# Routed expert products on one core: the last nine tiles done by halves of their outputs

## The reference, cut to what matters

```python
y      = einsum('bct,bcd->bdt', x, cond_w[itok])          # 64 blocks of 64x64, 4096 rows of 1024
logits = y @ W_gate + b_gate                              # 8 experts
_, top = top_k(logits, 2)                                 # two experts for each row
y_all  = relu(einsum('bsd,edh->bseh', y, W_e) + b_e)      # 1024 x 1024 for each expert
out    = x + take_along_axis(y_all, top, 2).mean(axis=2)
```

## Time and profile before

| what | value |
|---|---|
| median of 3 runs | 889.98 us (889.56 to 890.32) |
| the profiled execution, its own time | 888.81 us |
| its span in the trace | 887.1 us |
| PE busy | 851.0 us, 96% of the span |
| POOL busy | 446.5 us, 50% |
| DVE busy | 428.5 us, 48% |
| ACT busy | 256.9 us, 29% |
| DMA | 162.47 MB, 200 GB/s of memory traffic over the span |

### The profile page before, as it was taken

One profiled execution on the slowest core, in us unless ns is written; L12 is line 12 of the kernel. 1 busy time (PEld: TensorE's weight loads), 2 busy tenths in 40 slices (PEclk: granted clock), 3 DMA queues, 4 the chain that ended last, 5 costly groups with the idle time before them and its releaser, 6 DMA issues.

```text
span 887.1 us, 16691 instructions
## 1 busy us (share of the span) xinstructions
PE 851.0 (96%) x4154; PEld 674.1 (76%) x4155; DVE 428.5 (48%) x578; ACT 256.9 (29%) x310; POOL 446.5 (50%) x500
## 2 busy tenths in 40 slices
PE   7788899999999999999999999999999999999993
PEld 4344468888888888888888888888888888888883
DVE  6698876847643373335533373336433733333320
ACT  5555412134522252114311331115111511111220
POOL 3002224366566647654665556555655565555411
PEclk9899999999999999999999999999999999999997
DMA  9999698998965686547754594547664655444433
GB/s 335 418 415 351 227 330 265 341 333 251 288 158 109 130 266 136 106 95 196 200 103 93 98 298 101 107 100 213 171 118 95 189 114 109 91 101 97 82 48 47
DMA packets 51034, 162.47 MB, mean 183 GB/s; under 512 B 11594, under 2 KB 11658, under 8 KB 50986
## 3 DMA queue, kind: packets, MB, share of 16 engines
q0 software_dynamic: 24544, 76.74, 40.4%
q1 hardware_dynamic: 20618, 67.79, 21.0%
q10 hardware_dynamic: 5840, 17.57, 5.0%
HBM read 106.74 MB, written 70.52 MB: 200 GB/s over the span
## 4 chain that ended last, share of the span: by engine, by line
PE 88%; DVE 6%; DMA 2%; issue 2%; ACT 1%; ACTq 0%; POOL 0%; DVEq 0%; POOLq 0%
PE psO L606 85%; DVE turned L855 2%; PE psO L547 2%; DMA y_rows<-ys 1%; ACT ys L699 1%; DMA raw<-in_L_cond_weights 1%; DVE w_lo L868 1%; PE psG L559 0%; DVE run_hot L918 0%; DVE place_hot L910 0%; DVE idx_all L884 0%; DVE idx_all L883 0%; DVE idx_all L886 0%; DVE raw L885 0%; PE psL L571 0%
## 5 line engine op out<-in xcount | busy, mean ns | idle before, releaser
L606 PE MATMUL psO<-w_hi,a_hi 128*128 (+1 forms) x1104 | 341.7, 391 | 0.3 <-issue 0.3
L606 PE MATMUL psO<-w_lo,a_hi 128*128 (+1 forms) x1104 | 340.6, 390 | 0.0
L606 PE MATMUL psO<-w_hi,a_lo 128*128 (+1 forms) x1104 | 340.4, 390 | 0.0
L464 POOL DMA_INDIRECT rows<-y_rows,idx_g x248 | 255.7, 1031 | 106.8 <-issue 52.1
L606 PEld LDWEIGHTS psO<-w_hi,a_lo 128*128 128x128 f32 x1104 | 207.5, 188 | 43.4
L606 PEld LDWEIGHTS psO<-w_lo,a_hi 128*128 128x128 f32 x1104 | 207.6, 188 | 43.3
L606 PEld LDWEIGHTS psO<-w_hi,a_hi 128*128 128x128 f32 x1104 | 206.9, 188 | 44.1 <-issue 1.7
L1031 DVE TENSOR_TENSOR a_lo<-ys,a_hi 128x1024 fp32r<-128x1024 f32 x62 | 75.9, 1224 | 115.6 <-ACT a_hi L735 115.6
L723 ACT ACTIVATE ys<-ys 128x1024 f32<-128x1024 f32 x33 | 35.0, 1061 | 258.1 <-DVE ys L993 258.1
L723 ACT ACTIVATE rows<-rows 128x1024 f32<-128x1024 f32 x33 | 35.0, 1061 | 252.7 <-DVE rows L993 252.7
L993 DVE TENSOR_TENSOR ys<-psO,bias 128x1024 f32<-128x1024 f32 x33 | 40.2, 1219 | 124.6 <-PE psO L606 108.3
(11 more groups left out here) (141 smaller groups left out, 337.4 us busy)
## 6 DMA issues: line engine op xcount, KB each, us to landing
raw<-in_L_ffn_W_e SPq DMA_DIRECT2D x56, 512.0 KB, 6.2
y_rows<-ys ACTq DMA_DIRECT2D x32, 512.0 KB, 8.3
out<-in_x SPq DMA_DIRECT2D x14, 1024.0 KB, 9.3
rows<-in_x SPq DMA_DIRECT2D x16, 512.0 KB, 10.1
more_x<-in_x SPq DMA_DIRECT2D x16, 512.0 KB, 11.0
bias<-in_L_ffn_b_e SPq DMA_DIRECT2D x8, 512.0 KB
rows<-y_rows,idx_g POOLq DMA_INDIRECT x248
raw<-in_L_ffn_W_e POOLq DMA_DIRECT2D x4, 512.0 KB, 9.0
```

The source lines that it names most:

```text
L464: pool.indirect_dma_start(out=rows[:, slot, a * DQ:(a + 1) * DQ], out_offset=None, in_=y_parts[0:(1 + TOK) * Q, :], in_offset=bass.Indirec ...
L606: last = nc.tensor.matmul(ps[:, h * BANK:(h + 1) * BANK], a[:, p, k * P:(k + 1) * P], w[:, bass.ds(slot + (k * H + h * BANK), BANK)], star ...
```

## The change

Tiles 60 to 68 (HALVED = SURE - 4 = 60 and up) are done by halves of the outputs. PE does all 24 matmuls of half 0 and reports (s_half), then the 24 of half 1. DVE adds the bias to one half as soon as it is there, ACT rectifies it, and POOL scatters it: 128 pieces of 2 KB for each half, with indices 2i and 2i + 1 into `out` seen as rows of 512. POOL makes these in two small operations, waits for the first half's rectifier, issues its scatter, **waits for that to land** (s_add1), waits for the second half's rectifier and issues its scatter, whose landing counts in s_add as before. PE's loop that asks whether a tile is there now begins at 60; it began at 64.

```diff
+    HALVED = SURE - 4
+    out_halves = out.rearrange("n (h c) -> (n h) c", h=NH)
+        idx_h = sb("idx_h", [P, 2 * OS], U32)
+                def scatter_halves(t):
+                    n, half, m = t
+                    pool.wait_ge(s_add, n * 16)
+                    c = pool.value_load(tile_c[0:1, bass.ds(n, 1)], min_val=0, max_val=COLS - 1)
+                    nc.gpsimd.tensor_copy(idx_s[:, m:m + 1], idx_row[:, bass.ds(c, 1)]).then_inc(s_ixs, 1)
+                    pool.wait_ge(s_ixs, n - (EARLY - 1))
+                    pool.sem_inc(s_step, 1)
+                    nc.gpsimd.tensor_scalar(idx_h[:, m:m + 1], idx_s[:, m:m + 1], 2.0, None, ALU.mult).then_inc(s_ixh, 1)
+                    nc.gpsimd.tensor_scalar(idx_h[:, OS + m:OS + m + 1], idx_s[:, m:m + 1], 2.0, 1.0, ALU.mult,
+                                            ALU.add).then_inc(s_ixh, 1)
+                    pool.wait_ge(s_ixh, (n - (HALVED - 1)) * 2)
+                    pool.sem_inc(s_step, 1)
+                    pool.wait_ge(s_out1, n - (HALVED - 1))
+                    pool.sem_inc(s_step, 1)
+                    pool.indirect_dma_start(
+                        out=out_halves, out_offset=bass.IndirectOffsetOnAxis(ap=idx_h[:, m:m + 1], axis=0),
+                        in_=o_sb[m][:, 0:BANK], in_offset=None, compute_op=ALU.add).then_inc(s_add1, 16)
+
+                    pool.wait_ge(s_add1, (n - (HALVED - 1)) * 16)
+                    pool.sem_inc(s_step, 1)
+                    pool.wait_ge(s_out, n + 1)
+                    pool.sem_inc(s_step, 1)
+                    pool.indirect_dma_start(
+                        out=out_halves, out_offset=bass.IndirectOffsetOnAxis(ap=idx_h[:, OS + m:OS + m + 1], axis=0),
+                        in_=o_sb[m][:, BANK:D], in_offset=None, compute_op=ALU.add).then_inc(s_add, 16)
...
                 with pool.Fori((SURE - 4) // 4, (NT + 3) // 4, 1) as i:
...
-                                                  scatter(tile(i, c))))
+                                                  scatter_halves(tile(i, c))))
...
-                                for h in range(NH):
+                                for h in hs:
...
-                    products(t, psO[m % 2], e, slot)
+                    if halves:
+                        for h, done in ((0, s_half), (1, s_mm)):
+                            products(t, psO[m % 2], e, slot, hs=range(h, h + 1), done=done)
+                    else:
+                        products(t, psO[m % 2], e, slot)
...
+                def relu_halves(t):
+                    n, half, m = t
+                    for h, before_it, after_it in ((0, (s_bo1, n - (HALVED - 1)), s_out1), (1, (s_bo, n + 1), s_out)):
+                        at = slice(h * BANK, (h + 1) * BANK)
+                        act.wait_ge(*before_it)
+                        nc.scalar.activation(o_sb[m][:, at], o_sb[m][:, at], ACTF.Relu, scale=0.5).then_inc(after_it, 1)
...
+                def finish_halves(t):
+                    n, half, m = t
+                    e = needed(n)
+                    dve.wait_ge(s_add, (n - (OS - 1)) * 16)
+                    dve.wait_ge(s_bias, e * 16 + 16)
+                    for h, before_it, after_it in ((0, (s_half, n - (HALVED - 1)), s_bo1), (1, (s_mm, n + 1), s_bo)):
+                        dve.wait_ge(*before_it)
+                        V.tensor_tensor(o_sb[m][:, h * BANK:(h + 1) * BANK], psO[m % 2][:, h * BANK:(h + 1) * BANK],
+                                        bias[:, bass.ds((e % 2) * H + h * BANK, BANK)], ALU.add).then_inc(after_it, 1)
```

More of the change, by code:

```diff
@@ L226, in build @@
         s_from = sem("s_from")
+        s_half, s_bo1, s_out1, s_add1, s_ixh = sem("s_half"), sem("s_bo1"), sem("s_out1"), sem("s_add1"), sem("s_ixh")
         s_run, s_fill2, s_list = sem("s_run"), sem("s_fill2"), sem("s_list")
@@ L593, in ranks, with products @@
                     last.then_inc(s_rank, 1)
-                def products(t, ps, e, slot, ks=range(KD), hooks={}):
+                def products(t, ps, e, slot, ks=range(KD), hooks={}, hs=range(NH), done=s_mm):
                     n, half, m = t
@@ L611, in products @@
                     if ks[-1] == KD - 1:
-                        last.then_inc(s_mm, 1)
+                        last.then_inc(done, 1)
                 def early_products(t, ks=range(KD), hooks={}):
@@ L622, in early_products, with all_products @@
                     products(tile(0, t), psO[t % 2], 0, 0, ks, hooks)
-                def all_products(t):
+                def all_products(t, halves=False):
                     n, half, m = t
@@ L666, in _ @@
                 all_products(tile(0, EARLY))
-                with pe.Fori(2, SURE // 4, 1) as i:
+                with pe.Fori(2, HALVED // 4, 1) as i:
                     for c in range(4):
@@ L670, in _ @@
                 there = guard(pe)
-                with pe.Fori(SURE // 4, (NT + 3) // 4, 1) as i:
+                with pe.Fori(HALVED // 4, (NT + 3) // 4, 1) as i:
                     for c in range(4):
-                        there(i * 4 + c, lambda: all_products(tile(i, c)))
+                        there(i * 4 + c, lambda: all_products(tile(i, c), halves=True))
             @block.scalar
@@ L793, in ahead, with step @@
                         act.reg_add(reg, reg, 1)
-                def step(i, c, run):
+                def step(i, c, run, last=relu):
                     v = i * 4 + c
                     run(v - 1, lambda: (run(v, lambda: parts(tile(i, c))),
-                                        needed(v - 1), relu(tile(i, c - 1)),
+                                        needed(v - 1), last(tile(i, c - 1)),
                                         run(v, lambda: ahead(v))))
@@ L811, in _ @@
                     for c in range(4):
-                        step(i, c + 1, there)
+                        step(i, c + 1, there, relu_halves)
                 split_to(2 * (E - 1))
@@ L1122, in finish_last, with step @@
                     finish(t, e)
-                def step(i, c, run):
+                def step(i, c, run, last=finish_last):
                     v = i * 4 + c
@@ L1127, in step @@
                                                         run(v + 1, lambda: returned(tile(i, c + 1))))),
-                                        finish_last(tile(i, c - 1)),
+                                        last(tile(i, c - 1)),
                                         run(v, lambda: ahead(v))))
@@ L1148, in _ @@
                     for c in range(4):
-                        step(i, c + 1, there)
+                        step(i, c + 1, there, finish_halves)
                 split_to(2 * (E - 1))
```

## The result

The changed kernel takes **925.0 us** (median of 4 runs, 923.4 to 928.2), the one before 889.8 (889.4 to 890.3). The ratio is 1.041, 95% interval [1.0395, 1.0432]: slower, 35 us of it. The forecast was 920, range 906 to 932.

What follows compares the result with a forecast made beforehand. PE bounds the kernel before; after the change POOL does from tile 60, with 13 exposed landings of 4.0, 18 issues of 1.6, 9 index rounds of 1.75 and 4 gathers of 6.2 us: 920 us, range 906 to 932.

Steps and rivals of the forecast that it cites:

- POOL becomes the bound: From tile 60 on, POOL needs more per tile than PE's 10.88 us and never catches up.
- 13 exposed landings of 4.0: POOL's waits for half scatters to land, 4.0 us each, range 3.4 to 5.3; halving saves 1.3.
- Rival (c): Landing is fixed cost, mostly latency: a half takes 4.7 or more, 9 us more, 929; chance 13%.
- Issues of 1.6: POOL's 18 issues of half scatters take 1.6 us each, ends 1.0 and 2.0.
- Rival (b): POOL's issue costs by bytes or rows, 1.1 in place of 1.6, with quicker waking: 13 us less, 907; chance 20%.
- Indices 1.75: POOL, index copy to issue: 1.75 us with two more small operations and a semaphore round, bounds 1.5 and 1.9.
- Tiles with a gather 15.15, without 12.95: POOL's us per tile behind tile 60: 15.15 for tiles 61 to 64, 12.95 for those without a gather.
- rival (d): POOL's issues slowed by DVE beside them: 0.5 us on nine issues, 4.5 more, 925; chance 8%.
- PE 0, and DVE and ACT halves 0.69 and 0.63: PE's order by halves costs 0; each half bias takes about 0.69 us, each half rectifier about 0.63.
- Late gathers just in time: Tile 68's gather comes late, its a_lo done by 859; PE needs it at 862.6, so PE keeps pace.
- The tail, 7.3 behind the last issue: From the last issue's end to the span's end: 8.63 less 1.3 for the shorter transfer, 7.3 us.
- The gain meant, 2.3 us: Last tile's tail: 1.0 us from half bias and rectifier, 1.3 from a shorter last transfer, if POOL is free.

Runs made afterwards that it cites:

- e3: Kernel before with only the scatter split in two, both behind the full rectifier, the second behind the first's landing: 923.4 us, ratio 1.039.
- e4: The changed kernel, but half 0's landing is waited for ahead of the next tile's indices, not ahead of half 1's issue: 891.5 us, ratio 1.003.
- e1: Kernel before with only PE's matmuls of tiles 60 to 68 ordered by halves and its guard from tile 60: 888.2 us, ratio 0.999.
- e9: Kernel before with 14 guards on POOL behind its last scatter, for which nothing waits: 892.8 us, ratio 1.002.
- e11: Kernel before with 56 guards on POOL behind its last scatter: 898.6 us, ratio 1.008.
- e2: The changed kernel with PE, bias and rectifier by halves, but one full scatter a tile: 887.5 us, ratio 0.998 to before.
- e8: The version of e2 timed again in more rounds: 887.0 us, ratio 0.999 to before.
- e10: The changed kernel with each half's scatters in their own chain, SP asking at the end whether first halves landed: 891.9 us, ratio 1.001.
- e7: The changed kernel with each half's scatters in their own chain, POOL asking at the end in 14 guards: 889.3 us, ratio 1.002.
- e6: The change, its wait between halves too, for tile 68 alone: 892.5 us, ratio 1.004 to before.

## Why the prediction was right, point by point

- **POOL becomes the bound**: right. e3 has the whole loss with nothing but the scatter split, and e4 takes it away with one wait moved.
- **13 exposed landings of 4.0**: 13 were seen, 4.24 between halves and 4.0 ahead of copies; 54.2 us in place of 52. A full landing before took 5.2 to 5.5, so halving saved 1.1 (between halves) to 1.4 (ahead of copies), about the 1.3 read from the flow of the data. The wait between halves is the longer of the two, where the prediction's low end had it as the shorter. The split by the Trainium skill, "DMA: Bandwidth & Descriptors" (Anatomy of one DMA), 0.6 saved and 4.7 left, isn't what the trace shows. Rival (c), the landing as a fixed cost of 4.7 or more, falls with these 4.0 to 4.2.
- **Issues of 1.6**: right. First halves 1.62 to 1.78, second 1.56 to 2.17. Rival (b), an issue that costs by its bytes, falls: 2 KB rows cost what 4 KB rows do.
- **Indices 1.75**: right for eight tiles (1.68 to 1.75 from copy to issue), 2.57 for tile 60, where the copy itself took 1.00 (it began while DVE's a_lo was running).
- **Tiles with a gather 15.15, without 12.95**: 15.6 and 13.1. Of the 2.5 us that the four tiles with a gather are over, 1.0 is the landings, 1.0 two second issues of 2.05 and 2.17 which began while DVE's a_lo was running (863.52 and 863.03 in the rows above): rival (d), in a small size. The gather's own part, 25.0 in place of 4 x 6.2, is right by luck: it began 0.6 us before the end of the issue ahead of it and not 0.45 behind, but its copy took 0.8 in place of 0.2 and two of its issues, beside a_lo as well, 1.95 and 1.64.
- **PE 0, and DVE and ACT halves 0.69 and 0.63**: right; 0.687 and 0.632 are the means after, and e1 shows PE's 0.
- **Late gathers just in time**: right, but with 0.9 us in hand (a_lo of tile 68 at 864.26, PE due at 865.2) where the prediction had 3.6 (859 against 862.6).
- **The tail, 7.3 behind the last issue**: this step failed. It is 8.4 (918.14 to 926.5). The data did end earlier: the rows below are half microseconds behind the last issue (columns as in the earlier trace rows), three of after, where the flow is over by 920.8, 2.7 us behind the issue, and one of before, where it is over by 882.4, 3.9 behind. So 1.3 us of transfer are saved, and the end comes only 0.3 earlier. That POOL's queue has a share in the end is shown by e9 and e11; why 8.4 are left, where that queue alone would leave 7.5, is not.

```profile
918.50:919.00 0.50, 0.00 (x0) 0.00 (x0) 0.00 (x0) 0.00 (x0) 0.00 (x0) 0.50 1.16 66
...
920.00:920.50 0.50, 0.00 (x0) 0.00 (x0) 0.00 (x0) 0.00 (x0) 0.00 (x0) 0.50 1.00 180
920.50:921.00 0.50, 0.00 (x0) 0.00 (x0) 0.00 (x0) 0.00 (x0) 0.00 (x0) 0.50 0.16 25
```

```profile
882.00:882.50 0.50, 0.00 (x0) 0.00 (x0) 0.00 (x0) 0.00 (x0) 0.00 (x0) 0.50 0.21 33
```

The profiled span is 7.9 us over the sum of 918.6. By place: 2.6 are there before tile 60 is reached (784.19 of the earlier trace rows is 786.82 here), 1.1 at tile 60 itself, 2.5 in the four tiles with a gather, 0.6 in the rest of the chain, 1.1 in the closing. The first is a matter of this execution in part: its 928.2 is the longest of the four runs. None of the prediction's signs of being wrong showed: POOL waits for ACT at no half issue of tiles 65 to 68, and the pairs stand 5.75 us apart or more.

The gain meant, 2.3 us, was also too large by its second part: 1.0 from bias and rectifier is there (e2, e8), the 1.3 from a shorter last transfer mostly isn't (e10: 1.3 in all, where 2.3 was named).

## What to carry to other kernels

Before a transfer is split, count the waits that its issuer will stand in: each piece that must land before the next is issued costs the whole way there and back, here 4.2 us for half the data where the full one had 5.4, and an engine at 50% busy time can be full. Waits belong in chains, each piece behind the one that it really conflicts with (e7, e10), and as late in the queue as the conflict allows (e4). And what stands behind the last issue on POOL's queue delayed the end of the program, even where nothing waited for it (e9, e11).

## What the runs showed of the hardware that was not expected

- The accumulating indirect DMA takes POOL 1.6 us to issue for 128 rows, of 2 KB or of 4 KB; the gather of 128 rows of 1 KB takes 1.0. In the traces of before and after, from 500 us on, longer ones (up to 2.4 and 2.0) are found only where the issue began while one of DVE's subtractions (a_lo, w_lo) was running; all others took 1.56 to 1.67 and 0.94 to 1.04.
- Behind the end of POOL's last issue the span has 8.5 to 8.6 us with a full scatter (before, e1, e2) and 8.0 to 8.4 with a half one (the change, e3, e4, e6, e10), though the half's data end 1.3 us earlier behind the issue. Each guard put behind it adds about 0.16, and a landing waited for there adds 5.6. What the 8 us consist of stays open.
- The first 310 us, up to the bias of tile 16, end up to 5 us apart from profile to profile (305.79 to 310.89), though no version changes what is done there, and the tiles behind stand 10.88 apart; the medians of the kernel before go from 888.6 to 892.3 over three chips. Differences of 0.1% can't be read from whole times of this kernel, only from stretches of the trace.
